# One transformer block on one core: the middle four of eleven pipelined iterations written out instead of looped

## The reference

```python
mod = (silu(c) @ wmod).reshape(8, 6, 1, -1)      # sa, ca, ga, sb, cb, gb
h = layernorm(x) * (1 + ca) + sa
x = x + ga * attention(h)                        # 16 heads of 16 features, softmax over 512 keys
h = layernorm(x) * (1 + cb) + sb
shared = gelu(h @ shared_up) @ shared_down       # 2 experts, every token
gate = the 4 largest of softmax(h @ router_w.T), zero elsewhere
routed = (gelu(h @ routed_up) * gate) @ routed_down   # 16 experts, all computed
x = x + gb * (shared + routed)
```

## Time and profile before

| | us |
|---|---|
| median of 3 runs | 1054.28 |
| lowest and highest run | 1052.84, 1055.86 |
| the profiled execution: device time | 1056.11 |
| the profiled execution: span from first to last instruction | 1054.3 |
| TensorE busy | 944.9 (90% of the span) |
| VectorE busy | 680.8 (65%) |
| ScalarE busy | 630.9 (60%) |
| GpSimd busy | 380.2 (36%) |

### The profile page before, as it was taken

The page is one execution under the profiler, slowest core; times in us unless marked ns, Lnnn a source line. Parts: engine busy times, 40 slices in busy tenths (PEclk is TensorE's granted clock), DMA queues, the critical chain, the costliest instruction groups (busy, mean ns, idle before and its releaser), DMA issues.

```text
span 1054.3 us, 17394 instructions
## 1 busy us (share of the span) xinstructions
PE 944.9 (90%) x5928; PEld 423.4 (40%) x5928; DVE 680.8 (65%) x1315; ACT 630.9 (60%) x1033; POOL 380.2 (36%) x325
## 2 busy tenths in 40 slices
PE   5468887899999999999999899999999999997897
PEld 3112222234444354444434354444444444345564
DVE  5675576766876677676866676676866667724333
ACT  3145553676675758666776657666675757662343
POOL 4331222232432434243434333243434332344354
PEclk9657988899999999999999998999999999999899
DMA  6810600172016210442017200452017100320130
GB/s 208 180 45 29 117 2 0 46 168 101 1 36 170 68 61 11 140 83 101 1 42 191 85 20 1 123 110 101 1 36 195 64 19 1 111 65 37 66 122 21
DMA packets 50428, 78.53 MB, mean 74 GB/s; under 512 B 8216, under 2 KB 44568, under 8 KB 46240
## 3 DMA queue, kind: packets, MB, share of 16 engines
q1 hardware_dynamic: 50336, 77.36, 27.0%
HBM read 64.31 MB, written 12.89 MB: 73 GB/s over the span
## 4 chain that ended last, share of the span: by engine, by line
PE 78%; DVE 9%; ACT 3%; issue 3%; DMA 2%; POOL 2%; SPq 1%; DVEq 0%; POOLq 0%; ACTq 0%
PE scalar_bank L840 21%; PE down_bank L978 20%; PE pv_bank L912 12%; PE vector_bank L889 12%; DVE neg_max L783 5%; PE scalar_bank L889 5%; PE vector_bank L840 4%; PE scalar_bank L923 2%; PE vector_bank L931 2%; ACT probs L591 1%; DVE rows L657 1%; POOL act_lo L547 1%; PE vector_bank L896 1%; DMA probs<-in_router 1%; DVE o_raw L830 1%
## 5 line engine op out<-in xcount | busy, mean ns | idle before, releaser
L783 DVE TENSOR_REDUCE neg_max<-vector_bank 128x1 f16<-128x512 f32 x512 | 339.7, 688 | 140.2 <-PE vector_bank L889 130.4
L591 ACT ACTIVATE probs<-scalar_bank 128x512 f32<-128x512 f32 x512 | 291.1, 603 | 207.4 <-PE scalar_bank L889 204.6
L547 POOL TENSOR_TENSOR act_lo<-gelu,act_hi 128x512 f16<-128x512 f32 x144 | 178.0, 1256 | 202.8 <-ACT act_hi L581 192.9
L889 PE MATMUL vector_bank<-k_aug,q_aug 64*128 64x512 f16 x512 | 193.6, 411 | 40.7 <-DVE neg_max L783 23.3
L889 PE MATMUL scalar_bank<-q_aug,k_aug 64*128 64x512 f16 x512 | 199.4, 404 | 8.4 <-ACT f_ring L564 3.7
L978 PE MATMUL down_bank<-down_hi,act_hi 128*128 128x256 f16 x576 | 163.2, 283 | 0.3
L978 PE MATMUL down_bank<-down_lo,act_hi 128*128 128x256 f16 x576 | 159.6, 277 | 0.0
L978 PE MATMUL down_bank<-down_hi,act_lo 128*128 128x256 f16 x576 | 159.4, 277 | 0.0
L773 DVE TENSOR_TENSOR gelu<-gelu,gates 128x512 f32<-128x512 f32 x128 | 113.1, 903 | 61.8 <-ACT gelu L636 60.1
L912 PE MATMUL pv_bank<-probs,v_aug 128*32 128x512 f32 x1024 | 135.0, 639 | 0.0
L636 ACT ACTIVATE gelu<-scalar_bank 128x512 f32<-128x512 f32 x144 | 85.2, 597 | 78.5 <-PE scalar_bank L840 56.4
(11 more groups left out here) (122 smaller groups left out, 1107.9 us busy)
## 6 DMA issues: line engine op xcount, KB each, us to landing
gates<-gates_by_expert SPq DMA_DIRECT2D x32, 1024.0 KB, 5.1
q_aug<-q_parts SPq DMA_DIRECT2D x48, 128.0 KB, 3.9
k_aug<-k_parts SPq DMA_DIRECT2D x48, 128.0 KB, 7.5
x_pre<-in_x SPq DMA_DIRECT2D x8, 512.0 KB, 6.4
x_post<-in_x SPq DMA_DIRECT2D x8, 512.0 KB, 4.1
out<-x_post SPq DMA_DIRECT2D x8, 512.0 KB, 3.2
gates<-in_w_up SPq DMA_DIRECT2D x4, 576.0 KB, 11.7
gates<-in_w_down SPq DMA_DIRECT2D x4, 576.0 KB, 5.4
```

Of the source, the lines that this page charges most:

```text
L547: pool.tensor_tensor(act[1][:, c, :], gelu[:, n % NGELU, :], act[0][:, c, :], ALU.subtract).then_inc(s_elo, 1)
L591: scalar.activation(probs[:, n % U, :], src[:], ACT.Exp, scale=SCALE).then_inc(taken[kind], 1)
L783: dve.tensor_reduce(neg_max[:, (u // 2) % TT, at:at + 1], src[:], AX.X, ALU.max, negate=True).then_inc(done, 1)
L889: pe.matmul(dst[:], st[at:at + 64, pair, t * P:(t + 1) * P], mo[at:at + 64, pair, :], start=True, stop=True).then_inc(sig, 1)
```

## The change

The loop and the two lists beside it become one Python loop over all eleven iterations, so the program holds each of iterations 3 to 6 in full, with numbers in all waits.

```diff
@@ -309,12 +309,7 @@
         def iterations(eng, body):
 
 
-            for i in (-1, 0, 1, 2):
-                body(i, i % 2)
-            with eng.Fori(0, 2) as j:
-                body(j * 2 + 3, 1)
-                body(j * 2 + 4, 0)
-            for i in (7, 8, 9):
+            for i in range(-1, B + 2):
                 body(i, i % 2)
```

## The result

The changed kernel takes 1046.35 us (median of 7 runs, 1043.56 to 1051.56) beside 1054.28 us for the kernel before (7 runs, 1052.21 to 1058.84). The ratio is 0.9927, 95% interval 0.99 to 0.9954: faster by 7.9 us, with 4.9 to 10.5 inside the interval. The profiled execution took 1043.56 us, with a span of 1041.8.

The account below looks back on a forecast made before the run. TensorE, busy 90% of the span, was taken to bound the kernel, so only its idle time could be won. Branch 5.09 + entry 0.19 + registers 0.78 = 6.06 us off the median 1054.28 gives 1048.2 us, range 1045.0 to 1051.5.

Parts of the forecast that it names:

- The sum: Whole kernel: branch back, entry and registers together save 6.06 us from the median of 1054.28, giving 1048.2 us.
- The branch back: End of iteration 4, stretch of 35.40 us: removing the loop's branch saves 5.09 us, bounds 3.59 and 5.23.
- the sign: Profile after: the stretch from iteration 4's last mark to iteration 5's first takes 30.2 to 30.6 us.
- 2.63 + 0.96 + 1.50: At the branch back: 2.63 us VectorE's stall, 0.96 TensorE's own "issue" gap, 1.50 the low clock.
- The entry: Stretch holding the entry into the loop, 30.55 us against 30.17: saves 0.19 us, between 0 and 0.38.
- Registers: Register instructions of L162 and added semaphore counts, iterations 3 to 6: saves 0.78 us, bounds 0 and 1.24.
- The code itself: Unrolled program: more code in memory, but straight code is fetched ahead; costed at nothing.
- The slow clock: First stretch of iteration 5, 32.37 us against 29.85: not the branch's doing, taken as 0, ends +2.52 and -2.52.
- The branch is not what VectorE waited for: Rival: the gap is a late fetch caused by the load of gates; only 0.97 us left, 1053.3; chance 0.05.
- straight code runs dry: Rival: VectorE's fetch comes late in new unrolled code, 2.63 us each time; four give 1058.7, slower; chance 0.03.
- The clock takes it back: Rival: after the shift other places fall to the low clock, 2.52 us each; two more give 1053.3; chance 0.10.

Follow-up runs that it names:

- the repeat: The changed kernel run once more, unaltered, beside the kernel before at 1054.0 us: 1046.91 us, ratio 0.9923.
- the one with registers: The changed kernel, but iterations 3 to 6 compute every value waited for from a register as in the loop, no branch: 1045.91 us, ratio 0.9905.
- the one with the hint: The kernel before, loop on all engines, with a first instruction in the loop naming the branch's target ahead of time: 1046.91 us, ratio 0.9915.
- The two single loops: The changed kernel with the loop of before kept on one engine: VectorE alone 1049.65 us (ratio 0.9943), TensorE alone 1049.91 us (0.996).
- the kernel without the gate loads: The kernel before with two of the four gate loads cut to 8 of 512 columns: one run, 1050.78 us beside 1054.77.
- `head_slot` 0: The loop on TensorE alone, its first instruction meant to lie at the start of a block of code: one run, 1047.61 us beside 1054.77.

## Why the prediction was right, and where its steps were not

**The sum.** Forecast were 1048.2 us and a gain of 6.06; measured, 1046.35 and 7.9, then 7.1 in the repeat. By the traces at full clock the change is worth 6.3 us: 35.40 - 30.01 = 5.39 at the branch, and 0.93 of entry and registers (below). The other 0.8 to 1.6 us of the medians is within their intervals, and no run assigns it to anything. Two other kernels show the same and more clearly: by medians the one with registers gains 9.4 us and the one with the hint 8.4, where the way from the first mark of iteration 2 to that of 7 is shorter by 4.00 and 6.02 us in their profiles. Their runs have a mean granted clock of 0.950, those of the kernel before on the same chip 0.944. So the clock is the likeliest place; it is not shown where in the kernel it is lost.

**The branch back, forecast 5.09.** The total holds at 5.39; the stretch is 30.01 us, a little under the 30.2 to 30.6 named as the sign. The mechanism holds too: with the code at hand the branch is free, with a hint most of the stall goes, without the loop all of it. What failed is the split "2.63 + 0.96 + 1.50", read as three prices to be added. It describes what one chain passed through. TensorE's own gap was 0.96 only in the shadow of VectorE's stall, and 2.60 by itself. It also hung on the load of the gates, without which it was gone. Had the change taken VectorE out of the loop alone, my prices would have promised 2.63 of the 5.09 or more, and it would have brought 5.39 - 4.90 = 0.49 by these stretches. The step at fault is the sentence that the 0.96 us "is one more 'issue' gap, on TensorE itself": it was the visible end of a fetch under way. That 5.09 came near 5.39 all the same is no luck: the change took away all stalls at once, and the three numbers add up along one chain.

**The entry, forecast 0.19.** It is 30.55 - 30.00 = 0.55, above my upper end of 0.38. I took the difference to 30.17, the last stretch of an odd iteration with registers, for the entry's price, though that stretch is itself 0.17 longer than the 30.00 it takes with constants. The kernel with registers and no loop also has 30.55 there, so the price is not one of the loop's branches. The two single loops have 30.39 and 30.17 there, VectorE's and TensorE's part.

**Registers, forecast 0.78.** Two of its steps fail in opposite directions. After the change odd and even iterations are alike, so parity had no part in it, and the 30.17 in front of iteration 4 was a cost of 0.17 that I had called normal. It is not the register waits by themselves: the kernel with the hint has the same waits and takes 30.00 there, and the one with registers takes 30.17 in front of iteration 4 and 30.00 in front of iteration 6. Where it is 30.17 in these two and in the kernel before, VectorE idles 0.50 or 0.51 us ahead of one aggregation, where it is 30.00 only 0.15. The line is from the kernel before; what VectorE waits for in the 0.35 us stays open.

```profile
497.22 0.38 DVE L651 BATCH_NORM_AGGREGATE mean_var<-stats 128x2 f32<-128x6 f32 x4 [0.50 <-DVE stats L647]
```

And I excluded a gain, wrongly: the first stretch of iteration 3 was 29.85 with registers and is 30.18 with constants. The kernel with the loop on ScalarE, GpSimd and SyncE alone has 29.88 and 29.87 in its iterations 3 and 5, so it comes with theirs; how, I haven't traced. Summed over the stretches of iterations 3 to 6 at full clock (that of iteration 5 taken from the kernel without the gate loads, 29.83), the looped form costs 0.38 us beside the branch and the entry; with the entry, 0.93 against 0.97 forecast. The sum was right by luck: the errors cancelled.

**The code itself, at nothing.** Right. In the changed kernel no stretch at full clock is longer than its like in iteration 2 by more than 0.01 us, and there is less to fetch: 47 + 29 packets of instructions in place of 51 + 41, which fits the register instructions being gone. That the code comes ahead of its use shows in the last but one stretch of iteration 4, 571.20 to 595.95: a packet of q8 falls in it, at 582.62, and TensorE is busy for 24.75 of its 24.75 us.

**The slow clock, 0 with 2.52 to either side.** The place is right, and so is the reason for taking 0: in the profile after, iteration 5 lost 0.17 us and iteration 6 1.74. The 2.52 stands, now as 2.54: its partner, the same stretch at full clock, was 29.83 in the kernel without the gate loads.

**The rivals.** "The branch is not what VectorE waited for" is out by the loop with two of the gate loads cut, though the load does delay TensorE's second block; "straight code runs dry" by all straight kernels. "The clock takes it back" did not happen in the medians, but single runs of the changed kernel reach 1051.56. That something beyond branching had to be paid, as I read from the 3674 ns of TensorE's branch, holds: it is over 15 times the 233 ns of TensorE's taken branch whose target is at hand, while VectorE's takes 63 ns in both cases and waits behind it.

## What to carry to other kernels

A loop with a long body can pay for fetching its start again when it branches back, here 5.4 us for the one branch back, and nothing for the branch itself. Unrolling took all of it away, a hint at the loop's head 4.28 us. `head_slot` 0 took 3.88 of the 4.90 us that TensorE's loop costs alone; with the loop on all engines it was not run. A gap in a chain of waits is the price of its cause only if no other engine was late at the same time: before taking one cause away alone, look at what the next engine was doing in the meantime. And where one iteration of a kernel is already in the form that a change gives to all, compare stage by stage, but don't take the other iterations' stretches for the norm.

## What the runs showed of the hardware

- A taken branch to code that isn't at hand held TensorE's sequencer for 3.4 to 3.7 us in the four kernels whose TensorE has the loop without a hint, and left 2.85 to 3.18 us between VectorE's branch and its next step; the same branch with a hint 0.48 us and 0.51; one to the instructions just before it took 63 ns on VectorE and 233 on TensorE.
- A second wait of 2.60 us follows on TensorE nine matmuls behind the branch's target, with the loop on TensorE alone. It is gone with `head_slot` 0, and in the kernel before it (0.96 us) is gone without the load of the gates.
- An idle array need not slow the clock at once. With VectorE's loop alone, TensorE was busy 0.02 of the 2.00 us from 605.00 on, and the granted clock stayed at 1.00; in the kernel before, 0.57 of 2.00 us from 604.80 on was followed by 3.50 us at a mean clock of 0.51. That 1.00 and 0.51 are levels of about 2.4 and 1.2 GHz is an estimate from the same trace, with one column a cycle assumed: matmuls of 256 columns (L978) start every 0.11 us at 1.00 (318.10, 318.21, 318.32), and at the low clock three of them start at 608.01, 608.20 and 608.41 and the next matmul at 608.63, 0.21 us each. The stretches of the kernel with VectorE's loop alone, columns as in rows 3:

```profile
605.00:607.00 2.00, 0.02 (x1) 0.02 (x1) 0.77 (x2) 0.00 (x0) 0.00 (x0) 1.00 1.02 422
607.00:609.00 2.00, 1.98 (x12) 1.09 (x13) 1.62 (x4) 0.60 (x1) 0.00 (x0) 1.00 0.90 297
```

- The same code took 279.72 and 283.54 us to the first mark of iteration 2 in two executions of the changed kernel; whole times scatter by 8 us (1043.56 to 1051.56). Changes of a few us have to be read from stretches at full clock.
